# Layer 2's node steps of a four-layer graph network: their order on three engines

## The reference

```
h   = relu(layernorm(x))
hn  = h @ W_node.T + b_node
ef  = ssp(ssp(edge_attr @ W_e1.T + b_e1) @ W_e2.T + b_e2)     # ssp = softplus - log 2
agg = segment_sum(hn[src] * ef, dst)
x   = x + ssp(agg @ W_fc1.T + b_fc1) @ W_fc2.T + b_fc2
h3  = relu(layernorm(x))                                      # input of layer 3
```

## Time and profile before

| | us |
|---|---|
| median of three timed runs | 4206.68 |
| lowest, highest | 4205.99, 4207.88 |
| the profiled execution's own time | 4208.87 |
| its span, first to last instruction | 4207.6 |
| last gather of layer 2 issued at | 3054.50 |
| first gather of layer 3 issued at | 3102.64 |

### The profile page before, as it was taken

The page is one execution under the profiler, slowest core; times in us unless marked ns, Lnnn a source line. Parts: engine busy times, 40 slices in busy tenths (PEclk is TensorE's granted clock), DMA queues, the critical chain, the costliest instruction groups (busy, mean ns, idle before and its releaser), DMA issues.

```text
span 4207.6 us, 67388 instructions
## 1 busy us (share of the span) xinstructions
PE 2442.4 (58%) x13316; PEld 2042.1 (49%) x13316; DVE 2599.9 (62%) x7231; ACT 1818.6 (43%) x4182; POOL 3014.1 (72%) x3188
## 2 busy tenths in 40 slices
PE   2666666655556666666444444444656666666667
PEld 1455455554445555555444334444545554554556
DVE  4444444443566666667544444344559999999998
ACT  3444444421344444432211111112447887877875
POOL 3777777777677777777477777777747777777764
PEclk8778888776687888877656666666768999889988
DMA  4444444432344344432233333333456222222221
GB/s 132 110 124 118 121 124 116 122 90 66 88 121 124 114 124 118 121 104 68 78 104 107 105 109 104 109 109 109 115 106 119 57 57 57 57 57 58 57 47 31
DMA packets 238975, 405.80 MB, mean 96 GB/s; under 512 B 66706, under 2 KB 137515, under 8 KB 238572
## 3 DMA queue, kind: packets, MB, share of 16 engines
q0 software_dynamic: 99968, 207.33, 20.4%
q10 hardware_dynamic: 78736, 125.09, 10.5%
q1 hardware_dynamic: 59868, 69.07, 5.3%
HBM read 332.15 MB, written 67.78 MB: 95 GB/s over the span
## 4 chain that ended last, share of the span: by engine, by line
POOL 48%; issue 27%; SPq 10%; DMA 7%; DVE 4%; PE 2%; ACT 2%; ACTq 0%; DVEq 0%; POOLq 0%
POOL t_work L675 48%; DMA t_work<-d_T,t_tabG 6%; SPq L636 6%; SPq L702 4%; ACT t_acc L306 0%; PE ps L1914 0%; DVE t_acc L1883 0%; DVE ps L1371 0%; DVE t_x L1946 0%; DVE t_x L986 0%; PE ps L1337 0%; DVE t_halves L837 0%; DVE t_dev L299 0%; DMA t_tabG<-in_wgt 0%; ACTq L224 0%
## 5 line engine op out<-in xcount | busy, mean ns | idle before, releaser
L675 POOL DMA_INDIRECT t_work<-d_T,t_tabG x3116 | 2943.5, 945 | 1072.6 <-issue 922.3
L1337 PE MATMUL ps<-t_work,t_acc 128*128 x2592 | 450.1, 333 | 445.4 <-SPq L734 424.4
L1337 PEld LDWEIGHTS ps<-t_work,t_acc 128*128 128x128 f32 x2592 | 401.2, 238 | 518.7 <-issue 518.2
L1398 DVE TENSOR_TENSOR t_acc<-t_acc,ps 128x128 f32 (+1 forms) x732 | 210.6, 288 | 668.3 <-PE ps L559 342.7
L1387 DVE TENSOR_TENSOR t_hT<-t_work,ps 128x512 f32<-128x512 f32 x244 | 167.3, 686 | 510.8 <-ACT ps L1474 510.6
L1474 ACT COPY ps<-t_acc 128x512 f32 x244 | 140.5, 588 | 788.7 <-SPq L734 781.5
L1337 PE MATMUL ps<-t_hT,t_acc 128*128 128x128 f32 x1296 | 268.6, 392 | 289.6 <-DVE t_acc L1398 285.4
L1337 PEld LDWEIGHTS ps<-t_hT,t_acc 128*128 128x128 f32 x1296 | 252.5, 298 | 307.7 <-DVE t_hT L1387 301.8
L592 ACT ACTIVATE t_acc<-ps,t_bcol 128x1024 f32<-128x1024 f32 x98 | 109.1, 1113 | 660.0 <-DVE ps L605 654.1
L1774 PE MATMUL ps<-t_work,t_hT 128*128 x1960 | 324.0, 315 | 92.7 <-DVE t_acc L1784 77.6
L1337 PE MATMUL ps<-t_work 128*128 x1312 | 235.5, 342 | 243.6 <-SPq L734 221.0
(11 more groups left out here) (189 smaller groups left out, 4413.5 us busy)
## 6 DMA issues: line engine op xcount, KB each, us to landing
d_edge_net<-t_acc ACTq DMA_DIRECT2D x98, 512.0 KB
t_acc<-d_edge_net SPq DMA_DIRECT2D x98, 512.0 KB, 4.0
t_work<-d_T,t_tabG POOLq DMA_INDIRECT x3116
t_acc<-in_edge_attrT ACTq DMA_DIRECT2D x96, 512.0 KB, 4.2
t_acc<-d_T SPq DMA_DIRECT2D x1280, 0.5 KB
t_acc<-d_T SPq DMA_DIRECT2D x640, 0.5 KB
t_work<-d_T SPq DMA_DIRECT2D x640, 0.5 KB
t_acc<-d_T ACTq DMA_DIRECT2D x12, 790.1 KB, 15.6
```

Source lines behind the costliest of these rows:

```text
L675: pool.indirect_dma_start(out=work[:, at:at + width], out_offset=None, in_=table, in_offset=bass.IndirectOffsetOnAxis(ap=idx[:, g * QUAD + ...
L1337: last = pe.matmul(sums(layer, s, width), masks[s % MASKS][:, k, :], rows_k, start=(k == 0), stop=(k == QUAD - 1))
L1398: dve.tensor_tensor(out=o, in0=o, in1=sums(layer, s, width), op=ALU.add).then_inc(e_acc[layer], 1)
```

## The change

VectorE: in each iteration of layer 2 the control words and additions come first, then the node steps of the iteration, then masks and multiplies. The steps `centre_rows`, `finish_f1`, `add_f2` and `keep_h3` move one pair later; `keep_scores` keeps its pair. ScalarE: `spread_rows` and `finish_h3` move one pair later as well, and `spread_rows` goes from the iteration's end to ahead of `finish_h3` and the copies. `copy_h3` keeps its pair and now follows `finish_h3` of the same group in the same iteration. TensorE: `product_f2` keeps its pair but goes from ahead of `sum_pair` to behind it, `node_scores` and `turn_h3`. The waits that guard bank 7 are set to the new order. No instruction is added or removed.

```diff
@@ product_f2
-            passed_by(pe, s_scc, closed_by(CLOSED_AT[k] - 4))
+            passed_by(pe, s_scc, closed_by(CLOSED_AT[k] - 3))
@@ node_scores
-            pe.wait_ge(s_xs, BASE2 + closed_by(CLOSED_AT[k] + 3))
+            pe.wait_ge(s_xs, BASE2 + closed_by(CLOSED_AT[k] + 2))
@@ tensor_nodes2 (called ahead of sum_pair) is gone; in tensor_nodes2_behind:
             if closed_at(q - 5) is not None:
                 turn_h3(closed_at(q - 5))
+            if closed_at(q - 3) is not None:
+                product_f2(closed_at(q - 3))
             if closed_at(q - 1) is not None:
                 product_f1(closed_at(q - 1))
@@ vector_nodes2, now called behind the additions, ahead of masks and multiplies
-            if closed_at(p - 4) is not None:
-                centre_rows(2, closed_at(p - 4))
             if closed_at(p - 7) is not None:
                 keep_scores(closed_at(p - 7))
-
-        def vector_nodes2_behind(p):
-
-            if closed_at(p - 2) is not None:
-                finish_f1(closed_at(p - 2))
+            if closed_at(p - 5) is not None:
+                centre_rows(2, closed_at(p - 5))
             if closed_at(p - 3) is not None:
-                add_f2(closed_at(p - 3))
-            if closed_at(p - 5) is not None:
-                keep_h3(closed_at(p - 5))
+                finish_f1(closed_at(p - 3))
+            if closed_at(p - 4) is not None:
+                add_f2(closed_at(p - 4))
+            if closed_at(p - 6) is not None:
+                keep_h3(closed_at(p - 6))
@@ scalar_nodes2
             if closed_at(p - 4) is not None:
-                finish_h3(closed_at(p - 4))
+                spread_rows(2, closed_at(p - 4))
             if closed_at(p - 5) is not None:
+                finish_h3(closed_at(p - 5))
                 copy_h3(closed_at(p - 5))
             if closed_at(p) is not None:
                 copy_lap2(closed_at(p))
             if closed_at(p - 1) is not None:
                 soft_f1(closed_at(p - 1))
-            if closed_at(p - 3) is not None:
-                spread_rows(2, closed_at(p - 3))
```

More of the change, by code:

```diff
@@ L1254, in store_h3 @@
             st_s.add(act.dma_start(scores.rearrange("(t p) q -> p t q", p=P)[:, lo:hi, :], score8[:, lo:hi, :]))
-        def tensor_nodes2(q):
-            if closed_at(q - 3) is not None:
-                product_f2(closed_at(q - 3))
         def tensor_nodes2_behind(q):
@@ L1344, in sum_groups @@
                     tensor_nodes1(p)
-                if layer == 2:
-                    tensor_nodes2(p)
                 if p < PAIRED:
@@ L1423, in mask_groups @@
                     vector_nodes1(p)
-                if layer == 2:
-                    vector_nodes2(p)
                 if p <= PAIRED:
@@ L1435, in mask_groups @@
                     vector_nodes1_behind(p)
+                if layer == 2:
+                    vector_nodes2(p)
                 if layer == 0 and p in FLOAT_AT:
@@ L1454, in mask_groups @@
                             multiply(2 * p + 4 + j, slot)
-                if layer == 2:
-                    vector_nodes2_behind(p)
                 if layer == 0 and p - 2 in NODE_AT:
```

## The result

The changed kernel took 4214.13 us (median of 17 runs, 4211.83 to 4218.02), the kernel before 4206.83 in the same sessions (17 runs, 4204.90 to 4209.93). The ratio is 1.0017, with an interval of 1.001 to 1.0023: slower by 7.3 us, where +10.8 was forecast. The time lies in the predicted range, at the lower edge of the forecast's own spread (4214 to 4221) and next to the rival with cheap TensorE steps (4209 to 4214). It is just under the 8.4 us (0.2%) that counted as telling it from no change. So the interval leaves no doubt about the sign, but the size falls in the class within 0.2%, to which I had given 0.25, and not in "slower", which had 0.71.

What follows compares the result with a forecast made beforehand. Gathers were taken to pace the loop, node steps to set only the gap before layer 3. Loop 0 and legs +8.4, +2.7, -0.4, +0.1 sum to +10.8 us: 4206.7 becomes 4217.5, range 4210 to 4222.

Steps and rivals of the forecast that it cites:

- cheap TensorE steps: Rival for the end of layer 2: forecast mechanism at the faster TensorE clock, +2.2 to +7 us, 4209 to 4214; chance 0.14.
- slower: Outcome class for the whole kernel: a time above 4215.1 us, given 0.71.
- What bounds the kernel: Layer 2's loop goes at the gathers' pace; node steps set the time only in GpSimd's 47.19 us gap before layer 3.
- The loop: Layer 2's gather loop: multiplies up to 7.7 us behind their landing, cover of 15 us, so cost 0.
- the loop pays too: Rival in the gather loop: multiplies later than 15 us add 13 groups times 1 us, 4219 to 4232; chance 0.07.
- the gathers bound it all: Rival for the whole kernel: layer 3 takes up the loss, so nothing changes, 4206.7 us; chance 0.06.
- First leg: End of layer 2, last copy (step 243) to finish_h3 of group 8: 12.85 us in place of 4.4, +8.4.
- Second leg: End of layer 2, from finish_h3 of group 8 to that of 9: 14.45 us in place of 11.7, +2.7.
- The two bounds of the sum: End of layer 2: every TensorE step at the faster rows gives +2.2 us, at the slower rows +14.5.
- Third and fourth leg: End of layer 2: finish_h3 of 9 to that of 10, -0.4 us; from there to the last keep_scores, +0.1.
- The additions come earlier, and nothing gains by it: VectorE at layer 2's end: additions of pair 121 come 3 to 4 us earlier, without gain.
- the end gets shorter: Rival at layer 2's end: earlier additions of pair 121 gain 3.1 us through group 12's chain, 4203.6; chance 0.07.

Runs made afterwards that it cites:

- the version with the loop alone: Changed order only for node groups 0 to 4, groups 5 to 12 in the old order, against the kernel before: 4208.34 us, ratio 1.0004.
- The swap of the two TensorE steps: Changed kernel with product_f2 ahead of turn_h3 on TensorE, both still behind sum_pair: 4210.45 us, ratio 1.0006 against the kernel before.

## Why the prediction was right, and where it was off

**What bounds the kernel: right.** The loop goes at the gathers' pace in every version (the waits for SyncE in 2081 to 3056 us are 3.0 to 5.2 us in all), and every change of the gap came through to the time within the intervals: +7.5 gave +7.3, +7.4 gave +5.9, -0.5 gave +0.8, -2.9 gave -2.3, +1.8 gave +2.9, +4.4 gave +4.7, +6.8 gave +6.4, -16.5 gave -14.8 and -13.4 gave -15.4 (gap against 47.19, median against before's in the same session).

**The loop: right.** Waits of 4.3 us, 14 times, as before, and the version with the loop alone costs 0.8 us, with an interval that includes no change. The rival "the loop pays too" falls. So does "the gathers bound it all", since the gap grew and nothing took it up.

**First leg, +8.4: right in mechanism, and in size partly by luck.** It holds 7.7 of the 7.8 us of the sum. `finish_h3` of 7 is behind the copy, `turn_h3` of 7 waits for it (6.54 us), and `product_f2` of 8 stands behind that. The chain that ended last in the changed kernel passes through the very steps that I added up (start, us, step), from `turn_h3` of 7 to the store of 7:
```profile
3059.75 1.12 PE ps L1218 x4
3060.86 1.71 PE ps L1184 x8
3062.57 1.71 PE ps L1153 x2
3064.28 2.53 PE ps L1330 x16
3066.81 0.79 PE ps L1235 x8
3067.60 0.50 PE ps L1136 x4
3068.13 0.39 ACT t_acc L1144
3068.55 0.53 ACTq L1254
```
But `turn_h3` and `product_f1` came at the slow clock (1.12 and 1.71 us, where I had 0.6 and 0.9), while `product_f2`, `node_scores`, `turn_lap2` and the store were shorter than my 2.05, 1.2, 1.1 and 0.9. These errors cancel all but 0.75 us. The swap of the two TensorE steps gives back 2.2 us of the leg: 1.7 are `product_f2` of 8, which then runs while TensorE waits, and the rest goes with shorter sums behind it (2.05 us in place of 2.53). The other 5.5 are `finish_h3` of 7 behind the copy and `finish_h3` of 8 behind `copy_lap2` of 10 and the store. These stood in my sum as terms; as the cause I had named only `finish_h3` of 7 and `product_f2` of 8.

**Second leg, +2.7: the term that was mis-sized.** It measured +0.9. I took `product_f2` of 9 at 1.85 us and the other TensorE steps between the two levels. (Its faster price, 1.2 us, stands in no row; the changed kernel shows 1.06.) TensorE had the granted clock 1.00 from 3068 to 3076, so `product_f2` took 1.06 us, and the activations of group 10 began 4.6 us into the leg (3073.76) where my terms give 6.0: 1.4 less. In this leg the condition of the rival "cheap TensorE steps" was met, though over the whole gap its +2.2 to +7 was not. The store of group 8, for which I had 0.9 behind the activations of 11, had its issues beside their last one (3080.71 and 3081.12), and `finish_h3` of 9 came 0.55 behind it: 0.4 less. These 1.8 us are the larger part of the 3 between forecast and measurement; the scatter of a leg, up to 0.7 us, bears on them too. The two bounds of the sum, +2.2 and +14.5, did hold it; the value taken between them lay too near the slower end. The reason for that choice, more waiting and so a lower clock, was borne out only on average: granted 0.63 over the gap in place of 0.68, with 0.50 behind TensorE's wait of 6.54 us and 1.00 in the stretch that decided the second leg. By the rule of the Trainium skill (TensorE: Matmul & The Clock Gate, "Why this matters for your kernels") that gap would be followed by the half clock, and 3060 to 3064 agrees with it; taken for the whole chain, as the +14.5 did, it comes out 7 us too long.

**Third and fourth leg: right.** -1.0 and +0.1, with -0.4 and +0.1 forecast; the third was 0.55 us too long in my sum, which is within the scatter.

**"The additions come earlier, and nothing gains by it": right here, wrong in general.** They came 4.1 us earlier and the late order gained nothing (the version with them behind the node steps has no longer gap). In the old order the same move came with a gap 2.9 us shorter, of which the trace ties 1.7 to the move and the timing alone can't show any. The rival "the end gets shorter" named a gain of 3.1 us by them. It was refuted for the changed kernel, in which the additions no longer stand between `centre_rows` of 9 and `finish_f1` of 10. For the edit alone its size was near the measured one, but by another mechanism: not the chain of group 12 released earlier, but the additions out of the way of `finish_f1` of 10.

**What would show it.** I said 55 to 61 us for the gap, and it was 54.7; I said 8 to 13 us for all later marks, and behind the last copy they are 8.6, 7.6 and 7.8 late. `finish_h3` of 8 at 12.1 us and the additions, 4.1 earlier, are where I had them. I also said that a change of layer 3 by more than 2 us would speak against me. The profiled executions differ there by 2.7, and the ten kernels spread over 4.3. A pattern is hinted at: the three kernels in the old order have 1104.2 to 1105.0, four of the five in a late order 1100.7 to 1102.3, but the fifth has 1104.8. So whether the changed order shortens layer 3 is not settled by these runs. The medians speak for little of it: less the gap, they are 4160 to 4162 us in the old order and 4159 to 4161 in the late one, each uncertain by 3 to 4 us. One slip bears on nothing: TensorE's 28.35 us of 47 in the earlier trace rows are 60%, not 57%.

## What to carry to other kernels

Software pipelining that is free while transfers set the pace is paid where they end: price a lag of one step by writing out each engine's queue from the last landing on, and look there for operations that are ready but stand behind one that waits. At such a drain, order steps by the work that still hangs on them rather than by the loop's pattern; here that gained 15 us, twice what the change had lost. An edit with several parts can hide what one of them does: the additions' place went with a gap 2.9 us shorter on its own and did nothing beside the other moves, so take such an edit apart.

## What the runs showed of the hardware that I had not expected

The same few microseconds of matmuls cost up to twice as much by the clock that was granted when they came: 8 products of 128x128 took 1.92 and 1.06 us, 2 of 128x512 1.92 and 1.02, within 12 us of one trace. Which level a step meets changes with the order: the first leg's `product_f1` took 0.8 us more than I had planned from the old order's rows, and the second leg began 1.4 us sooner. The durations of one order's trace did not give those of the other.

GpSimd's gathers kept their pace over layer 2 in both orders of VectorE's queue: 779 of them took 0.94 us each in the mean, and 765 waited 233.5 us in total for their own issue, some 0.30 each, before and after.
